# A two-block transformer kernel on one core: the hardware loop over three batches written out in all five engines

## The reference, cut to what matters

```
m = silu(cond) @ w_ada + b_ada                      # nine shift / scale / gate rows per batch
h = ln(x)*(1+sc)+sh;  x += g * (window_attention(h) @ w_so + b_so)   # 16 heads, windows of 128, roll 64
h = ln(x)*(1+sc)+sh;  x += g * (topk_attention(h, ctx) @ w_co + b_co) # top 16 of 77 context keys
h = ln(x)*(1+sc)+sh;  x += g * (swiglu(h))          # 256 -> 2*1024 -> 256
nx = layer_norm(x)*gamma + beta
evidence = softmax(nx Wq (ctx Wk)^T / 16) @ (ctx Wv)
combined = [nx, evidence, cond]
routed = sum_e softmax(combined @ router_W)_e * (silu(combined @ e_w1[e]) @ e_w2[e])   # 3 experts
out = x + sigmoid(silu(combined @ gate_w1) @ gate_w2) * (routed @ out_w + out_b)
```

## Time and profile before

| | |
|---|---|
| median of 3 runs | 1477.76 us (1477.65 to 1478.56) |
| the profiled execution, its own time | 1480.46 us |
| its span, first to last instruction | 1478.3 us |
| TensorE busy | 1427.9 us (97%) |
| VectorE busy | 1013.9 us (69%) |
| ScalarE busy | 842.2 us (57%) |
| GpSimd busy | 316.9 us (21%) |

### The profile page before, as it was taken

One profiled execution on the slowest core, in us unless ns is written; L12 is line 12 of the kernel. 1 busy time (PEld: TensorE's weight loads), 2 busy tenths in 40 slices (PEclk: granted clock), 3 DMA queues, 4 the chain that ended last, 5 costly groups with the idle time before them and its releaser, 6 DMA issues.

```text
span 1478.3 us, 33113 instructions
## 1 busy us (share of the span) xinstructions
PE 1427.9 (97%) x9749; PEld 1201.2 (81%) x9749; DVE 1013.9 (69%) x4629; ACT 842.2 (57%) x2554; POOL 316.9 (21%) x517
## 2 busy tenths in 40 slices
PE   7968999999999999999999999999999999999987
PEld 5856888888888788888888788888888888887876
DVE  3484858677694867769595776959587685958532
ACT  3363374746656475665747466574757547574423
POOL 1523212121231212122132212213032211212100
PEclk9878999999999999999999999999999999999999
DMA  7600000010000000010010000000010000000000
GB/s 239 222 30 1 1 1 25 2 33 9 19 30 8 11 2 25 2 33 2 12 44 2 17 2 16 11 14 21 9 47 2 15 2 8 2 2 8 1 8 8
DMA packets 27222, 34.86 MB, mean 24 GB/s; under 512 B 3308, under 2 KB 22432, under 8 KB 26784
## 3 DMA queue, kind: packets, MB, share of 16 engines
q1 hardware_dynamic: 27039, 32.67, 7.0%
HBM read 28.44 MB, written 4.22 MB: 22 GB/s over the span
## 4 chain that ended last, share of the span: by engine, by line
PE 81%; DVE 12%; issue 4%; ACT 2%; DVEq 0%; SPq 0%; DMA 0%; POOL 0%; POOLq 0%; ACTq 0%
PE bank L921 14%; PE bank L946 11%; PE bank L876 10%; PE bank L928 7%; PE bank L749 6%; PE bank L808 5%; PE bank L885 4%; PE bank L796 4%; PE bank L860 3%; DVE knocked L2094 3%; PE bank L735 3%; PE bank L788 2%; PE bank L706 2%; DVE M L2082 2%; PE bank L720 1%
## 5 line engine op out<-in xcount | busy, mean ns | idle before, releaser
L876 PE MATMUL bank<-hB,Wm 128*128 128x256 f32 x1024 | 243.5, 384 | 4.1 <-issue 2.8
L876 PEld LDWEIGHTS bank<-hB,Wm 128*128 128x128 f32 x1024 | 191.1, 190 | 36.1 <-issue 12.1
L921 PE MATMUL bank<-nxT,W1nx 128*128 128x256 f32 x896 | 214.1, 385 | 0.0
L1331 ACT ACTIVATE prob<-bank,rmax 128x128 f32<-128x128 f32 x512 | 180.3, 434 | 31.2 <-DVE rmax L2042 31.2
L1338 ACT ACTIVATE probT<-bank 128x512 f32<-128x512 f32 (+1 forms) x256 | 141.7, 610 | 93.9 <-PE bank L860 78.0
L921 PEld LDWEIGHTS bank<-nxT,W1nx 128*128 128x128 f32 x896 | 167.8, 193 | 23.8 <-issue 2.8
L946 PE MATMUL bank<-W2p,gT 128*128 128x256 f32 x768 | 183.1, 382 | 0.0
L1674 POOL TENSOR_TENSOR scores<-scores,M 128x308 f32<-128x308 f32 x128 | 94.3, 736 | 332.9 <-DVE knocked L2094 332.9
L946 PEld LDWEIGHTS bank<-W2p,gT 128*128 128x128 f32 x768 | 143.6, 192 | 20.7
L1367 ACT ACTIVATE tbs<-bank,b1half 128x256 f32<-128x256 f32 x128 | 60.7, 474 | 147.6 <-PE bank L876 100.8
L1379 ACT ACTIVATE tbs<-bank,betaH 128x256 f32<-128x256 f32 x224 | 95.1, 485 | 83.0 <-PE bank L928 83.0
(11 more groups left out here) (219 smaller groups left out, 2620.9 us busy)
## 6 DMA issues: line engine op xcount, KB each, us to landing
Wm_g<-in_L_xcond_w_m_dram SPq DMA_DIRECT2D x4, 1024.0 KB, 5.5
W1ev<-in_L_xcond_e_w_dram SPq DMA_DIRECT2D x6, 512.0 KB, 6.8
x<-in_x_dram SPq DMA_DIRECT2D x16, 128.0 KB, 2.5
x<-in_x_dram SPq DMA_DIRECT2D x32, 64.0 KB, 2.8
Wm<-in_L_xcond_w_m_dram SPq DMA_DIRECT2D x1, 2048.0 KB, 9.2
out_dram<-acc SPq DMA_DIRECT2D x16, 128.0 KB, 1.7
out_dram<-acc SPq DMA_DIRECT2D x32, 64.0 KB, 2.0
batch_rows<-row_store SPq DMA_DIRECT2D x4, 384.0 KB, 3.8
```

Of the source, the lines that this page charges most:

```text
L876: m = pe.matmul(bank_of(name)[:, half * UT:(half + 1) * UT], Wm1[:, k, c:c + P], hB[:, k, :], start=(k == 0), stop=(k == CB - 1))
L921: pe.matmul(bank_of(name)[:, n * UT:(n + 1) * UT], W1nx[:, k, c0 + n * P:c0 + (n + 1) * P], nxT[:, k, :], start=(n == 0 and k == 0), stop= ...
L1331: m = act.activation(prob[:, s, i, :], psum[s][:, i * P:(i + 1) * P], ACT.Exp, bias=rmax[:, t, s * HPS + i:s * HPS + i + 1], accum_out=rsu ...
```

## The change

`with engine.Fori(0, NB - 1) as q` becomes `for q in range(NB - 1)` in each of the five engines' programs. The build then emits the twelve calls one behind the other, q is a Python number, and every value waited for and every address is a constant. No other line changes.

```diff
@@ sync
-            with sp.Fori(0, NB - 1) as b:
+            for b in range(NB - 1):
                 for r in range(1, UNITS + 1):
                     both(b * UNITS + r, r % UNITS, b)
                     load_x(b * UNITS + r + UNITS - 1, r - 1)
@@ tensor
             prologue()
-            with pe.Fori(0, NB - 1) as q:
+            for q in range(NB - 1):
                 for r in range(1, UNITS + 1):
                     both(q * UNITS + r, r % UNITS, q + r // 3)
             both(NU - 3, 1, NB - 1)
@@ scalar
-            with act.Fori(0, NB - 1) as q:
+            for q in range(NB - 1):
@@ gpsimd
-            with pool.Fori(0, NB - 1) as q:
+            for q in range(NB - 1):
@@ vector
-            with dve.Fori(0, NB - 1) as q:
+            for q in range(NB - 1):
```

## The result

The changed kernel took 1473.41 us in the median of 16 runs (1470.92 to 1479.46). The kernel before took 1482.17 us beside it (1477.58 to 1485.67, 16 runs, with the three shown ahead of the prediction among them). The ratio is 0.9953 with a 95% interval of 0.9940 to 0.9966: 5.0 to 8.9 us faster, 7 us by the ratio itself (the two medians alone lie 8.8 us apart). The forecast was 1477.76 - 8.0 = 1469.7 us, a ratio of 0.9946. That ratio lies in the interval. The time of 1473.41 us lies 0.5 us above the range, which ended at 1472.9.

A forecast was written before the change was run, and what follows sets the result against it. TensorE, busy 97% of the span, was taken to set the end. Terms 3.18 (turns) + 1.2 (r = 2) + 0.5 (r = 1) + 2.1 (r = 3) + 1.05 (r = 0) = 8.0 us gave 1469.7 us, range 1467.0 to 1472.9.

The forecast's parts named there:

- The turns: At the loop's two jumps back, TensorE waits for code to be fetched; removing them returns 1.92 and 1.26, together 3.18 us.
- r = 0: Three units in which the loop turns or exits: besides the jumps, 0.35 us each, 1.05 us (0.9 to 1.2).
- r = 2: Three units, loop against written-out k = 14: 0.39 us each, 1.2 us, partly VectorE's register instructions delaying L2101.
- only the turns: Rival: r = 2, 3 and 0 keep their stalls, transfers making r = 2's 0.39 us; 3.7 us gained, 1474.1 us, chance 7%.
- r = 3: Three units without a written-out counterpart: 0.7 us of stall each returned, 2.1 us (1.2 to 2.8).
- r = 1: Three units, loop against written-out k = 13: 0.19 and 0.18 us, 0.1 for the first, together 0.5 us gained.
- slower: Rival: straight code fetching falls behind, an engine 1.74 us late in each of twelve units; 1490.7 us, chance 2%.
- The sum: All terms over the two jumps and twelve units: 8.0 us saved, bounds 6.9 and 9.1.
- The time: Whole kernel: saving taken from the earlier median, 1477.76 - 8.0 = 1469.7 us, allowing some 0.5 us of scatter between runs.

The follow-up runs named there:

- e2: Changed kernel with three one-turn loops per engine, built into constants and branches to the next instruction; 1473.61 us, ratio 0.9952 to the kernel before.
- e3: Changed kernel with a two-turn loop round one semaphore instruction on TensorE at the two turn places; 1471.58 us, ratio 0.9950 to the kernel before.
- e5: Kernel before with TensorE's loop alone written out; second unit's start to k = 13 took 932.08 us, -4.18 against before.
- e6: Kernel before with all engines but TensorE written out; second unit's start to k = 13 took 933.25 us, -3.01 against before.
- e10: Kernel before, loop kept, with 22 overwritten matmuls where TensorE waits and some waits moved or added; 1475.72 us, ratio 0.9976 to the kernel before.
- e7: Kernel before with VectorE's loop alone written out; second unit's start to k = 13 took 932.89 us, -3.37 against before.
- e9: Changed kernel with 22 overwritten matmuls where TensorE waits and some waits moved or added; 1467.81 us, ratio 0.9925 to the kernel before.
- e8: Changed kernel with 64 more semaphore instructions at the start of VectorE's prologue; second unit's start to k = 13 took 929.24 us, -7.02 against before.

## Why the prediction was right and where it was wrong

**The turns.** Right in mechanism and nearly in size. The units with r = 0 gave 2.55 + 1.72 + 0.34 = 4.61 us; the prediction had 3.18 for the turns and 1.05 for their registers, 4.23 together. e2 and e3 show that the branch costs nothing beside a distant target, and e5 and e6 that only TensorE's own jump counts. The Trainium skill's page "Runtime: NRT & Kernel Launch", Instruction fetch mechanics, by which a taken branch out of the fetched blocks waits for its target, has the trace and the runs behind it here. The branch times of the Trainium skill's page "Advanced Engine Details and Errata", Control Flow Timing (51 and 108 ns), do not show as idle time at these places, since in e2 and e3 TensorE stands no measurable time; e2's compare-and-branches took 67 to 93 ns. They cannot explain branches of 3.26 and 3.91 us. What the prediction did not see is that its 1.74 and 1.08 us are what the issued matmuls left uncovered. The gaps vary with the branch: where e10 has 3.65 and 3.64 us for it, its units with r = 0 read 85.26 and 85.24 us, not 85.53 and 84.87.

**r = 2.** 1.2 us forecast, 0.40 + 0.55 + 0.54 = 1.49 measured. VectorE's loop is the cause of most of it, as L2101 in e5 and e7 shows; no jump falls into these units, and e2, which has near branches but constants, reads 82.24 us, so what is left of the loop is its register instructions. The rival "only the turns" fell with it: these units have the transfers of the loop (15 GB/s) and are as short as the written-out one.

**r = 3.** Mis-sized: 2.1 us forecast, 0.27 + 0.39 + 0.56 = 1.22 measured. I put most of the stall above the r = 2 unit down to the registers; it stays in straight code (TensorE is idle 0.28, 0.35 and 0.27 us in these units). With VectorE alone written out the three gave 0.52, 0.39 and 0.55 us, with TensorE alone 0.05 to 0.08.

**r = 1.** The step that failed in sign: "Together 0.5 us". Measured were -0.34, -0.34 and -0.01 us, 0.69 us lost. I read the cost from k = 13, one written-out unit, and took it for what every written-out unit of its kind would read. The 0.19 and 0.18 us did come, as TensorE's part (e5: 90.21 and 90.22 us), and VectorE's straight code took more than that away (e7: 90.86 and 90.58 us). The first unit's loss is not the clock's: at full clock in both it reads 90.40 us in e10 and 90.77 us in e9. Written out, VectorE has its six stops at other places, four of them in the units k = 1 and k = 5, both r = 1; the loop had put all of them into r = 3 and r = 0. That code position sets these places is what e8 shows; that a step into a new block is the reason is argued. The rival "slower" named late code in straight streams, but put it at 1.74 us an instance and on a short stream; what shows is 0.2 to 0.3 us, on VectorE.

**The sum.** The twelve units gave 4.61 + 1.49 + 1.22 - 0.69 = 6.63 us, against 8.0 forecast and just under the lower bound of 6.9. The profiled spans differ by 1478.3 - 1471.1 = 7.2 us, of which 0.35 is an earlier start of the first unit and 0.2 comes after k = 13.

**The time.** The step that put the result out of the range is the last one of the sum, "1477.76 - 8.0 = 1469.7". It carried the change over to the median of three runs that lay within 0.9 us of each other. Over 16 runs the kernel before has its median at 1482.17 us, 4.4 us higher, with a span of 8.1 us. With that median in its place the same step gives 1474.2 us, 0.8 us from the measured 1473.41. The three runs were three of the five lowest of the sixteen, and the profiled execution beside them, 2.7 us above their median, already showed more scatter than the 0.5 us. A range that was to hold an absolute time needed the scatter of whole executions, 6 us and more, and I had allowed 0.5 us. In the ratio the range was 0.9927 to 0.9967, and 0.9953 is within it, with some luck: the turns and r = 2 gave 0.67 us more than forecast, r = 3 and r = 1 gave 2.07 us less.

## What to carry to other kernels

Where an engine is busy 97% of the time and its loop turns over a long body (here 2378 recorded matmuls), look at the first instruction after each turn: a gap marked "issue" there is what writing the loop out returns, turn by turn, and a second copy of the body behind the loop shows in advance much of what else it will return, but not where short stops will fall in straight code (r = 1 here). Write out the loop of the bound engine first, then that of the engine it waits for; here those two gave everything. Measure an effect of 0.5% in windows between fixed points of the program, and quote an absolute time only with the scatter of many executions.

## What the runs showed of the hardware that was not expected

- A taken branch back over a few instructions took TensorE's stream 0.21 to 0.23 us and cost no idle time (e3). The jump back over four units took 3.3 to 3.9 us, of which issued matmuls hid all but 1.1 to 1.7 us. GpSimd's and SyncE's jumps over 248 and 123 instructions took 0.2 to 0.3 us.
- VectorE stops for 0.2 to 0.3 us now and then in straight code, with a packet of code on q14 0.7 to 0.9 us later. The same program stops at the same instructions in every execution: units repeat to 0.03 us.
- GpSimd's 128x2 tensor_tensor (L1668) took 0.71 us where it started just ahead of VectorE's L2118 and 1.10 us where it started just behind it; so in all eight of 832 cases that started inside a scalar_tensor_tensor of VectorE.
- A higher granted clock in a stretch does not shorten the whole by itself: e9's first unit is 1.6 us shorter and starts 1.6 us later after the same row of the prologue, while at the end the fillers gave 4.0 us.
- Executions of one kernel differ by up to 13 us, and in the profiles compared the difference was made in the first 60 us of the prologue, where TensorE was granted 0.83 to 1.00 of full clock from 25 to 45 us and 0.66 to 0.77 from 45 to 60 us.
